# Selective scan in a decoder block: alternate steps filled by a product with a diagonal, state sum by an identity product

## The reference, cut to what matters

```
def step(h, inp):
    u_t, dt_t, B_t, C_t = inp
    dA = exp(dt_t[:, :, None] * A)
    h = h * dA + (dt_t * u_t)[:, :, None] * B_t[:, None, :]
    y = einsum('bds,bs->bd', h, C_t)
    return (h, y)
y = y + u * D_skip
```

## Time and profile before

| what | value |
|---|---|
| median of three executions | 3817.49 us |
| the profiled execution's own time | 3814.09 us |
| span of its trace | 3812.3 us |
| TensorE busy | 3116.1 us (82%), 17860 matmul records |
| VectorE busy | 3388.7 us (89%) |
| ScalarE busy | 2703.3 us (71%) |
| GpSimd busy | 2585.8 us (68%) |
| mean granted TensorE clock | 0.894 of 2.4 GHz |

### The profile page before, as it was taken

The page is one execution under the profiler, slowest core; times in us unless marked ns, Lnnn a source line. Parts: engine busy times, 40 slices in busy tenths (PEclk is TensorE's granted clock), DMA queues, the critical chain, the costliest instruction groups (busy, mean ns, idle before and its releaser), DMA issues.

```text
span 3812.3 us, 50672 instructions
## 1 busy us (share of the span) xinstructions
PE 3116.1 (82%) x17860; PEld 2582.1 (68%) x17860; DVE 3388.7 (89%) x4041; ACT 2703.3 (71%) x6090; POOL 2585.8 (68%) x1216
## 2 busy tenths in 40 slices
PE   5777777778787888878787887888787888888999
PEld 3566666667676767667676776767676676777877
DVE  4999999998999999999999999999999999998100
ACT  5768687776878788777878778786777778676222
POOL 4778777776868677776777677776777678666000
PEclk7777677889898999989899899989999898999999
DMA  2111111112131222212231222312222121323344
GB/s 105 43 41 40 45 43 40 44 40 81 62 105 45 78 84 86 86 42 95 70 105 52 67 81 76 104 47 83 70 92 73 56 88 63 103 82 107 115 141 128
DMA packets 81490, 286.87 MB, mean 75 GB/s; under 512 B 9786, under 2 KB 10819, under 8 KB 80596
## 3 DMA queue, kind: packets, MB, share of 16 engines
q1 hardware_dynamic: 80210, 281.21, 22.5%
q10 hardware_dynamic: 1026, 2.42, 0.2%
HBM read 280.44 MB, written 3.15 MB: 74 GB/s over the span
## 4 chain that ended last, share of the span: by engine, by line
DVE 31%; POOL 27%; issue 24%; PE 13%; ACT 3%; DMA 2%; POOLq 0%; SPq 0%; DVEq 0%
POOL hC L613 24%; DVE h L835 23%; DVE psX L825 5%; PE psY L1067 4%; PE psG L1023 3%; POOL scratch L564 2%; PE psG L1094 2%; DMA wexp<-in_w_exp 1%; PE psX L1051 1%; ACT dA L803 1%; PE psX L1023 1%; POOL dtu L580 1%; DVE acc L885 1%; PE psX L1094 1%; ACT xs L777 0%
## 5 line engine op out<-in xcount | busy, mean ns | idle before, releaser
L613 POOL TENSOR_TENSOR hC<-h,cb 128x1024 f32<-128x1024 f32 x1024 | 2406.0, 2362 | 907.4 <-DVE h L835 815.3
L835 DVE TENSOR_TENSOR_SCAN h<-dA,psX 128x512 f32<-128x512 f32 x2048 | 2367.1, 1203 | 28.7 <-PE psX L1051 26.9
L803 ACT ACTIVATE dA<-dt,negA 128x255 f32<-128x255 f32 x4096 | 1726.8, 500 | 388.6 <-DVE h L835 385.7
L1067 PE MATMUL psY<-ident,hC 128*128 128x128 f32 x8192 | 1266.2, 305 | 419.9 <-POOL hC L613 368.0
L1067 PEld LDWEIGHTS psY<-ident,hC 128*128 128x128 f32 x8192 | 1061.2, 157 | 657.2 <-POOL hC L613 539.9
L825 DVE TENSOR_TENSOR psX<-dtu,psX 128x512 f32<-128x512 f32 x1384 | 949.3, 686 | 86.1 <-PE psX L1042 61.7
L1051 PE MATMUL psX<-ident,xs 128*128 128x128 f32 x2656 | 417.7, 310 | 84.2 <-DVE h L835 42.6
L1023 PE MATMUL psG<-x2T,wexp 128*128 128x256 f32 x1680 | 447.1, 395 | 24.9 <-DVE gl L961 9.9
L1094 PE MATMUL psG<-wexp,hid 128*128 128x256 f32 x1664 | 433.7, 385 | 20.5 <-DVE acc L885 12.5
L777 ACT ACTIVATE xs<-dtuT,bT 128x512 f32<-128x512 f32 x664 | 441.1, 716 | 0.2
L1051 PEld LDWEIGHTS psX<-ident,xs 128*128 128x128 f32 x2656 | 360.7, 162 | 106.5 <-ACT xs L777 54.2
(11 more groups left out here) (157 smaller groups left out, 1828.8 us busy)
## 6 DMA issues: line engine op xcount, KB each, us to landing
wexp<-in_w_exp SPq DMA_DIRECT2D x256, 512.0 KB, 3.6
cb<-c_dram SPq DMA_DIRECT2D x256, 512.0 KB, 3.7
xin<-in_xT SPq DMA_DIRECT2D x8, 256.0 KB, 4.2
w_in<-in_w_in SPq DMA_DIRECT2D x2, 1024.0 KB, 7.8
ctxT<-in_ctxT SPq DMA_DIRECT2D x8, 256.0 KB, 4.0
xrow<-in_x SPq DMA_DIRECT2D x8, 256.0 KB, 4.1
y<-acc SPq DMA_DIRECT2D x8, 256.0 KB, 3.4
w_x<-in_w_x SPq DMA_DIRECT2D x1, 1088.0 KB
```

Source lines behind the costliest of these rows:

```text
L613: eng.tensor_tensor(hC[i % NHC][:, :, :], h[i % NH][:, :, :], cw.to_broadcast([P, KI, L]), ALU.mult).then_inc(times_c, 1)
L803: made = eng.activation(dA[j % NA][:, c, 1:L], dt[n % 2][:, c, 1:L], ACT.Exp, scale=negA[:, JOBS[n][0], c, s:s + 1])
L835: eng.tensor_tensor_scan(h[i % NH][:, 2 * f:2 * f + 2, :].rearrange("p c t -> p (c t)"), dA[i % NA][:, 2 * f:2 * f + 2, :].rearrange("p c ...
L1067: made = eng.matmul(psY[:, tc, c * P:(c + 1) * P], hC[i % NHC][:, c, tc * P:(tc + 1) * P], ident[:, :], start=s == 0 and c == 0, stop=Fals ...
```

## The change

- `is_turned` becomes: odd steps above 12 (506 of 1024).
- A turned step: ScalarE makes two 128 x 128 diagonals of B (two instructions of 128 columns, two buffers), and TensorE multiplies the transposed dtu by them: 4 chunks x 2 time halves, eight matmuls of 128 x 128 that are not transposes.
- A plain step: VectorE's product is one instruction of 1024 columns.
- The sum over states: two matmuls with the identity as weights and 512 columns of hC each. psY keeps channels on partitions.
- The skip: four matmuls of 256 columns for each job, with a diagonal of D (made once for each layer) as weights; ScalarE's scaling of u goes.
- The turn of gT and its copy go: the gate's result is read by the projection as it is. The z branch is computed with channels on partitions, in twice as many matmuls of half the columns.
- TensorE's order within an iteration: fill of step i+1, then the sum of step i-2, then small work.
- The planner's constants: MM 440 to 280, TURN 125 to 150, a sum 1050 to 1100, a turned fill 1050 to 1100, a plain fill 240 to 280, the scaling 1270 to 600, and 300 instead of 60 between a piece and what depends on it.
- The context load moves on the SP queue to behind the second normalisation's place (and a first one to job 1's C copy).

```diff
 def is_turned(i):
-    return i % S % 3 == 2 and i > 12
+    return i % 2 == 1 and i > 12
...
-MM, TURN, EVICT, HALF_EVICT = 440, 125, 620, 470
-WINDOW, PE_OVER, FIRST = 24, 0, 1500
+MM, TURN, EVICT, HALF_EVICT = 280, 150, 620, 470
+WINDOW, PE_OVER, FIRST, HOP, NEAR = 24, 0, 1500, 300, 60
+SUM, SPREAD, OUTER, DIAG = 1100, 280, 1100, 600
...
-                    elif name == "turn" and part == 0 and JOBS[n][0] == 1:
-                        b = JOBS[n][1]
-                        on.wait_ge(normed[1], b)
...
+                    elif name == "norm2" and n + 1 < ROWS:
+                        load_context(n + 1)
...
-                    elif name == "skip":
-                        on.wait_ge(dtu_done, 2 * (n + 1))
+                    elif name == "skip_diag":
+                        on.wait_ge(set_up, SETUP + 1)
                         for c in range(KI):
-                            made = eng.activation(u[n % 2][:, c, :], u[n % 2][:, c, :], ACT.Identity,
-                                                  scale=dskip[:, JOBS[n][0], c:c + 1])
-                        made.then_inc(skipped, 1)
+                            made = eng.activation(skip_diag[:, n, c, :], ident[:, :], ACT.Identity, scale=dskip[:, n, c:c + 1])
+                        made.then_inc(skip_ready, 1)
...
+                        on.wait_ge(out_pair, weights_at(n, e, p) - 1)
...
                 for tc in range(KL):
-                    made = eng.activation(xs[:, tc, :], dtuT[n % 2][:, tc, :], ACT.Identity,
-                                          scale=bT[n % 2][:, tc, s:s + 1])
+                    made = eng.activation(b_diag[at % 2][:, tc, :], ident[:, :], ACT.Identity, scale=bT[n % 2][:, tc, s:s + 1])
                 made.then_inc(scaled, 1)
...
-                for f in range(2):
-                    on.wait_ge(times_b, 2 * PLAIN_TO[i] + f)
-                    eng.tensor_tensor(x[:, 2 * f:2 * f + 2, :], dtu[n % 2][:, 2 * f:2 * f + 2, :],
-                                      x[:, KI - 1:KI, :].to_broadcast([P, 2, L]), ALU.mult).then_inc(times_b, 1)
+                eng.tensor_tensor(x[:, :, :], dtu[n % 2][:, :, :], x[:, KI - 1:KI, :].to_broadcast([P, KI, L]),
+                                  ALU.mult).then_inc(times_b, 1)
...
                 for c in range(KI):
                     for tc in range(KL):
-                        made = eng.transpose(psX[i % 2][:, c, tc * P:(tc + 1) * P], xs[:, tc, c * P:(c + 1) * P], ident[:, :])
+                        made = eng.matmul(psX[i % 2][:, c, tc * P:(tc + 1) * P], dtuT[n % 2][:, tc, c * P:(c + 1) * P],
+                                          b_diag[at % 2][:, tc, :], start=True, stop=True)
...
                 on.wait_ge(times_c, i + 1)
-                for tc in range(KL):
-                    for c in range(KI):
-                        made = eng.matmul(psY[:, tc, c * P:(c + 1) * P], hC[i % NHC][:, c, tc * P:(tc + 1) * P], ident[:, :],
-                                          start=s == 0 and c == 0, stop=False, is_transpose=True, skip_group_check=True)
+                for f in range(2):
+                    made = eng.matmul(psY[:, 2 * f:2 * f + 2, :], ident[:, :], hC[i % NHC][:, 2 * f:2 * f + 2, :],
+                                      start=s == 0, stop=False, skip_group_check=True)
...
+                for c in range(KI):
+                    made = eng.matmul(psY[:, c, :], skip_diag[:, l, c, :], u[n % 2][:, c, :],
+                                      start=False, stop=True, skip_group_check=True)
...
-                if j > 0 and j % S == 0:
+                if i + 1 < STEPS:
                     fill_x(i + 1)
                 if j >= 0:
                     sum_states(j)
                     if j % S == S - 1:
                         add_skip(j // S)
-                if i + 1 < STEPS and not (j > 0 and j % S == 0):
-                    fill_x(i + 1)
```

More of the change, by code:

```diff
@@ L114, in tasks_turned @@
                 task("dtu_copy", n, tc, "ACT", EVICT, ("dtu_turn", n, tc), frees=("dtu_turn", n, tc))]
-    out.append(task("skip", n, 0, "ACT", 4 * HALF_EVICT, ("dtu", n, 1), ("c_copy", n, 0), ("b_hi", n, 0)))
+    if n == 0:
+        out += [task("skip_diag", l, 0, "ACT", 1200) for l in range(LAYERS)]
     return out
@@ L121, in tasks_post @@
     out = []
[L122 to L125, removed]
     if l == 0:
-        out += [task("next", n, 0, "PE", 4 * MM, *copied, opens="G"),
+        out += [task("next", n, 0, "PE", 4 * MM, ("gate", n), opens="G"),
                 task("next", n, 1, "PE", 4 * MM, ("next", n, 0)),
@@ L130, in tasks_post @@
     else:
-        out += [task("proj", b, 0, "PE", 4 * MM, *copied, opens="G"),
+        out += [task("proj", b, 0, "PE", 4 * MM, ("gate", n), opens="G"),
                 task("proj", b, 1, "PE", 4 * MM, ("proj", b, 0)),
@@ L233, in start @@
             return None, None
-        at = max([self.at[t.eng]] + [self.done[x] + 60 for x in t.needs])
+        at = max([self.at[t.eng]] + [self.done[x] + self.hop for x in t.needs])
         if not t.opens:
@@ L324, in loop @@
                 then = at["DVE"] + 1120
[L325 removed]
+                room = then - (OUTER if is_turned(i + 2) else SPREAD) + PE_OVER
                 limit = {"PE": room if i + 1 < STEPS else 1e12, "ACT": then + 500, "POOL": then + 600,
@@ L406, in decoder_block @@
         u = [sb(f"u{i}", [P, KI, L]) for i in range(2)]
-        sz = [sb(f"sz{i}", [P, KL, DI]) for i in range(2)]
+        sz = [sb(f"sz{i}", [P, KI, L]) for i in range(2)]
         dt = [sb(f"dt{i}", [P, KI, L]) for i in range(2)]
@@ L410, in decoder_block @@
         dtuT = [sb(f"dtuT{i}", [P, KL, DI]) for i in range(2)]
-        xs = sb("xs", [P, KL, DI])
+        b_diag = [sb(f"b_diag{i}", [P, KL, P]) for i in range(2)]
         bT = [sb(f"bT{i}", [P, KL, S]) for i in range(2)]
@@ L641, in small_work @@
                         on.wait_ge(gated, 2 * (n - 1))
-                        eng.activation(sz[n % 2][:, part, :], bank[k][:, :], ACT.Copy).then_inc(free[k], 1)
+                        eng.activation(sz[n % 2][:, 2 * part:2 * part + 2, :], two(k), ACT.Copy).then_inc(free[k], 1)
                     elif name == "tap":
@@ L841, in gate @@
                 if n > 0:
-                    on.wait_ge(full["G"], turn["turn", n - 1, 1][1] + 1)
+                    l, b = JOBS[n - 1]
+                    k, at = turn["proj", b, 0] if l else turn["next", n - 1, 0]
+                    on.wait_ge(full[k], at + 1)
                 if n + 1 < NJ:
@@ L1162, in small_work @@
                         made.then_inc(full[k], 1)
-                    elif name == "turn":
-                        k, dst = open_bank((name, n, part))
-                        on.wait_ge(gated, 2 * (n + 1))
-                        for i in range(2):
-                            for tc in range(KL):
-                                c = 2 * part + i
-                                made = eng.transpose(dst[:, i * L + tc * P:i * L + (tc + 1) * P], gT[:, tc, c * P:(c + 1) * P], ident[:, :])
-                        made.then_inc(full[k], 1)
                     elif name == "next":
```

101 lines of the change are left out of this document (47 added, 54 removed).

## The result

The changed kernel takes 4240.34 us (4238.97 to 4241.76, four runs) against 3816.15 (3812.71 to 3819.1): ratio 1.1112, 95% interval 1.1093 to 1.1131, so 11.1% slower. The forecast was 4225, range 4080 to 4450.

What follows compares the result with a forecast made beforehand. VectorE bounds the loop before and TensorE the tail; after, TensorE bounds throughout: 2584 + 1430 = 4014 us of work, plus start, tail, wait and clock terms, a span of 4222, forecast 4225 us, range 4080 to 4450.

Steps and rivals of the forecast that it cites:

- A float32 product leaves two records: TensorE's products: each issued float32 matmul leaves two records, so costs twice a transpose of the same columns.
- no dearer than transposes: Rival: identity and diagonal products leave one record per issued matmul, VectorE still bounds, 3511 us; chance 0.04.
- Sum +870: TensorE's sum over states: 1.72 us a step for 0.87, 1024 x 0.85 = +870 us.
- Fill +581: TensorE's turned fills: 506 at 1.72 us in place of 332 at 0.87, +581 us.
- Merged product 1.17: VectorE's plain step: one instruction takes 1.17 us, not 1.31, saving 73 us over 518 steps (bounds 0 and 140).
- ScalarE's diagonals 0.60 a step: ScalarE's scalings in turned steps: two instructions of 0.30 us, 304 us in all instead of 441, off the path.
- The clock: TensorE: more products mean more time at the upper clock level; 55 us charged for stretches at half clock.
- Head, tail and waits: Added to TensorE's work: +31 us at the start, +30, +10 and +7 in the tail, +75 for loop waits.
- 4014: TensorE's work in us after the change at full clock: 2584 before plus a net 1430.
- The new order costs nothing: Loop, fill ahead of sum: GpSimd's three buffers cover the later sum, cost 0.
- TensorE's sum is conserved: Planner puts more beside the steps than fits; this moves work out of the tail rather than adding any.
- The rival of coupling: Overfull steps make ScalarE, VectorE and TensorE wait for each other, 240 to 400 us for 75: 4390 to 4550; chance 0.14.

Runs made afterwards that it cites:

- The bf16 run: The changed kernel with hC and the identity of the sum in bf16, all else float32 as it was: 3628.1 us, 0.9505 of before.
- the diagonal fill alone: The kernel before with the fill of its 332 turned steps done by the diagonal product, and the plan moved with it: 3859.96 us, 1.0118 of before.
- the sum undone: The kernel before with the changed kernel's turned steps, diagonal fill and merged product, sum by eight transposes, old order, 300 ns planned everywhere: 4050.58 us.
- half the sum: The changed kernel with the sum over states done only for channels 0 to 255, except on a job's first step: 3752.23 us, 0.983 of before.
- a third turned: The changed kernel with only a third of its steps turned (332, as before) and 692 plain: 4438.13 us, 1.1628 of before.

## Why the prediction was right, point by point

- **The bound changes to TensorE, in the loop too.** Right: 99% busy beside experts, chain 83% TensorE, VectorE waiting 760 us for fills.
- **A float32 product leaves two records, each as dear as a transpose of its columns.** Right, and the core of the result: 4096 and 8096 records. The bf16 run shows that the bytes of psY and hC do not set the price. The rival "no dearer than transposes" fell at the point that was named.
- **Sum +870.** 1.71 us a step for 1.72. **Fill +581.** 1.78 us for 1.72: 506 x 0.06 = 30 us more. The prediction had bounds of 1.60 and 3.5 for it and chose near the lower one; that choice carried the forecast.
- **Merged product 1.17.** Measured 1.26, so 26 us and not 73 come off VectorE. It changed nothing, for VectorE no longer bounded. VectorE's busy time, named as a sign near 3080, is 3190.5; 47 of these 110 us are the merged product, the rest is not accounted for. **ScalarE's diagonals 0.60 a step** are 346.8 / 506 = 0.69, off the path as said.
- **The clock.** Granted 0.994; what the half-clock stretches cost is (1 - 0.994) x 4237 = 25 us, for 55. "More products, more time at the upper level" held in direction, here and with the diagonal fill alone (0.894 to 0.934). But more products are not needed for it. With half the steps turned by transposes, the stretch from 400 to 600 reads:

```profile
400.00:600.00 200.00, 139.16 (x875) 117.57 (x875) 180.22 (x161) 162.51 (x354) 154.93 (x72) 0.86 0.12 42
```

From 200 to 600 this kernel has 1538 records of transposes in its sums and fills, where the kernel before has 1304, and no more float32 products than that one. The granted clock is 0.89 and 0.86 in the two halves, where before it is 0.76 and 0.74, and TensorE is less busy (283 us for 298), not more. The diagonal fill on a third gives 0.85 there. So this stretch does not bear out the rule of the Trainium skill (TensorE: Matmul & The Clock Gate, Part 4: PE-mode transpose) that such transposes do not bring on the full clock, with which the prediction saw its rows agree. What raised the clock there these runs do not show.

- **Head, tail and waits.** TensorE is idle 4237 - 4120 = 117 us. 30 of them lie in the first 60 us, for 31; about 23 lie after 4000, for 47 of tail terms, part of which is slower records and not idle time; the 64 left are the loop's, for 75.
- **How near the total is** is in part luck. 4014 + 30 for the fill + 25 for the clock + 117 idle is 4186 of 4237 us; 51 us of TensorE's busy time are not accounted for. Clock and idle time came out 66 us under their terms, the fill and this rest 81 over: so the span is 15 off.
- **The new order costs nothing.** Understated: it gains. The prediction saw that a fill behind a sum is late, and gave the order no price; undoing it costs 141 us.
- **"TensorE's sum is conserved", so times add.** This held here only because the changed kernel's two engines are level without experts (5.9 to 5.75 us for two steps, in the prediction), so that TensorE is behind in every stretch. My expectations for the kernels with the sum undone, half the sum and a third turned used the same rule where it does not hold, and missed by 190 to 490 us. Tails that the sum of work does not see are a shown part of that; stretches bound in turn by one engine and the other are shown for the jobs without experts and argued for the rest.
- **The rival of coupling** (4390 to 4550) did not come in this kernel. Whether the planner's low constants cost anything was not tried. That changes of plan cost 110 to 160 us in a tail is shown, with as much expert work in it (431 against 275 us) or with more (412 against 299). The changed kernel's tail, 241 us, happened to be a good one.

## What to carry to other kernels

Count a matmul's cost by its columns, its records for each issued instruction and the start-to-start time, not by the mean busy time of a record: replacing float32 transposes by products with the identity or a diagonal may take fewer instructions (two for eight in the sum) or spare another engine (ScalarE here), and doubles TensorE's time for the same columns. When moving work between engines, compare them in each stretch, for a loop can pay the larger of the two in each. Read the tail by itself, and count what work was left to it: a plan that writes the order of a long loop can change the tail by over 100 us and leave the loop nearly as it was.

## What was not expected of the hardware

A float32 product of 128 columns runs as fast for its columns as one of 512 though each record loads its own weights: 1.78 us for sixteen against 1.71 for four of 512. And TensorE held full clock through a loop with 96 to 99% busy time, where the loop of before, 74 to 87% busy from 200 on, spent much of its time at the lower level (granted 0.74 to 0.96).
